# A new order of one turn in a two-layer Mamba, expert and attention kernel: feed-forward through bank 0, sums later, row transfers one by one

## What is computed

```python
xn = layernorm(x)
x = x + mamba(xn) + experts(xn)          # layer 0
xn = layernorm(x)
x = x + attention(xn) + swiglu_ffn(xn)   # layer 1

# mamba, per channel i (256) and state n (16)
hs, gate = split(xn @ in_proj.T)
u  = silu(conv4(hs) + conv_b)
dt, B, C = rmsnorm of the three parts of u @ x_proj.T      # 64, 16, 16 wide
dt = softplus(dt @ dt_proj.T + dt_b)
h[t, i, n] = exp(dt[t, i] * A[i, n]) * h[t-1, i, n] + dt[t, i] * u[t, i] * B[t, n]
y[t, i]    = sum over n of h[t, i, n] * C[t, n]
out = ((y + u * D) * silu(gate)) @ out_proj.T
# experts: the best one of 8 per token, 128 -> 512 -> 128 with relu
# attention: 16 heads of 8, window +-32; ffn: 128 -> 384 -> 128, silu(gate) * up
```

## Time and profile before

| | |
|---|---|
| time, median of 3 runs | 1080.61 us (1080.15 to 1082.40) |
| span of the profiled execution | 1078.4 us |
| busy in it: PE / DVE / ACT / POOL | 81% / 75% / 59% / 38% |
| turn 4 (scan 0 at 578.88 us, next turn's 109.05 us later): PE / DVE busy | 95 / 91 us |

### The profile page before, as it was taken

How to read it: one execution, slowest core, us unless ns; L and a number is a source line. 1 busy time by engine, 2 the same in 40 slices (tenths; PEclk the granted TensorE clock), 3 DMA queues, 4 the chain that set the end, 5 groups by cost and what they waited for, 6 DMA issues and landing times.

```text
span 1078.4 us, 14023 instructions
## 1 busy us (share of the span) xinstructions
...
## 2 busy tenths in 40 slices
...
DMA packets 85945, 123.09 MB, mean 114 GB/s; under 512 B 8560, under 2 KB 43760, under 8 KB 85744
## 3 DMA queue, kind: packets, MB, share of 16 engines
...
...
## 4 chain that ended last, share of the span: by engine, by line
PE 41%; DVE 30%; issue 13%; POOL 10%; ACT 4%; DMA 2%; SPq 0%; DVEq 0%; POOLq 0%
PE y_bank L1279 11%; DVE hst L801 10%; DVE dBu L793 5%; POOL hc L1190 3%; POOL xs_d L1158 3%; PE work L1297 3%; PE more L1398 3%; POOL x_res L1174 3%; DVE nmax L946 2%; PE work L1444 2%; PE work L1380 2%; DVE dc L863 2%; PE work_l L1380 1%; PE work L1410 1%; DVE fsg L955 1%
## 5 line engine op out<-in xcount | busy, mean ns | idle before, releaser
L1190 POOL TENSOR_TENSOR hc<-hst,bcr 128x1024 f32<-128x1024 f32 x116 | 277.6, 2393 | 507.2 <-DVE dBu L793 447.8
L1279 PE MATMUL y_bank<-hc,pk 128*128 128x512 f32 x512 | 261.4, 635 | 61.6 <-POOL hc L1190 48.1
L801 DVE TENSOR_TENSOR_SCAN hst<-dA,dBu 128x1024 f32<-128x1024 f32 x128 | 291.5, 2278 | 14.5 <-issue 12.6
L793 DVE TENSOR_TENSOR dBu<-dtu,bcr 128x1024 f32<-128x1024 f32 x128 | 176.3, 1377 | 15.4 <-DMA bcr<-bc_d 2.0
L1016 ACT ACTIVATE dA<-dt,neg_a 128x511 f32<-128x511 f32 x256 | 171.1, 727 | 9.3 <-DVE hst L801 8.0
L1279 PEld LDWEIGHTS y_bank<-hc,pk 128*128 128x128 f32 x512 | 92.3, 195 | 161.5 <-issue 77.9
L1101 ACT COPY pT<-more 96x512 f32<-96x512 f32 x120 | 69.8, 582 | 87.8 <-PE more L1398 87.6
L1398 PE MATMUL more<-pk,pexp 128*96 128x128 f32 x480 | 94.2, 292 | 21.0 <-ACT pexp L1088 16.2
L1398 PEld LDWEIGHTS more<-pk,pexp 128*96 128x96 f32 x480 | 57.8, 130 | 90.3 <-issue 71.2
L1088 ACT ACTIVATE pexp<-work,nmax 128x96 f32<-128x96 f32 x240 | 78.2, 339 | 15.4 <-DVE nmax L946 15.4
L1088 ACT ACTIVATE pexp<-work_l,nmax 128x96 f32<-128x96 f32 x240 | 78.1, 339 | 4.0 <-DVE nmax L946 3.8
...
## 6 DMA issues: line engine op xcount, KB each, us to landing
bcr<-bc_d SPq DMA_DIRECT2D x128, 512.0 KB
...
```

The source lines that it names most:

```text
L793: v.tensor_tensor(dBu[:], dtu[par], bcr[n % RING][:, 0:1, :].to_broadcast([P, NH, L]), ALU.mult).then_inc(s_dBu, 1)
L801: v.tensor_tensor_scan(hst[n % 2][:].rearrange("p h t -> p (h t)"), dA[n % 2][:].rearrange("p h t -> p (h t)"), dBu[:].rearrange("p h t -> ...
L1190: g_.tensor_tensor(hc[n % 2][:], hst[n % 2][:], bcr[n % RING][:, 1:2, :].to_broadcast([P, NH, L]), ALU.mult).then_inc(s_hc, 1)
L1279: last = t.matmul(y_bank[h][:], ident, hc[n % 2][:, h, :], start=False, stop=(n == N - 1))
```

## The change

The tables of the list are written anew and some units are split.

- `ffn` becomes `fg` (PE gate matmul and ACT tanh), `fs` (DVE), `fu` (PE up matmul) and `fh` (DVE), one slot or more apart, in slots 17 to 23 instead of three whole units at slots 12, 17 and 21. All six matmuls of a sequence go through bank 0 instead of the layer-1 banks; a new helper and a longer `take0` keep the order between them and the `pre` units.
- `zg0` and `zg1` go from slots 4 and 6 to slots 10 and 11, `sg0` and `sg1` to the heads of slots 11 and 12.
- `xdbl` to `dw` come earlier: `xdbl` slot 7 (was 9), `ss` slot 8 (10), `xdr` and `bc` slot 9 (12, 13), `dtT` 13 (16), `dtp0` 14 (18), `dtp1` 15 (19), `drl0`/`drl1` at the heads of 15 and 16 (19, 21), `de` 17 (22), `dw` 19 (23). `dt` moves from 25 to 24.
- A scan step is split into `step` (scan) and `product` (DVE `dBu`, POOL `hc`). Five units stand between the two (`MID`): `slots` at 3, `ss` at 8, `dw` at 19, `dt` at 24, `dtu` at 26.
- Steps 3 and 4 are one slot earlier (4 and 6). `sum` m now stands two slots after its step; for most m that is where it was, for m = 0, 9 and 12 one slot later, for m = 3 one earlier.
- `rows` is split: SP's load and DVE's copy of indices (`slots`) at slot 3, and the four indirect transfers at slots 5, 7, 9 and 11 instead of all at slot 10.
- `th0` is separated from `hs0` and moved behind the decays on ACT.

```diff
-PRE_AT = {0: ['xnT', 'hs0'], 2: ['u0'], 3: ['hs1'], 4: ['zg0', 'u1'], 6: ['sg0', 'zg1'], 7: ['sg1'], 9: ['xdbl'], 10: ['ss'], 12: ['xdr'], 13: ['bc'], 16: ['dtT'], 18: ['dtp0'], 19: ['drl0', 'dtp1'], 21: ['drl1'], 22: ['de'], 23: ['dw'], 24: ['dln'], 25: ['dt'], 26: ['dtu'], 27: ['start']}
-FFN_AT = {12: 0, 17: 1, 21: 2}
+HEAD = {11: [("pre", "sg0", 0)], 12: [("pre", "sg1", 0)], 15: [("pre", "drl0", 0)], 16: [("pre", "drl1", 0)],
...
+MID = {3: [("scan", "slots", 0)], 8: [("pre", "ss", 0)], 19: [("pre", "dw", 0)], 24: [("pre", "dt", 0)], 26: [("pre", "dtu", 0)]}
...
+SUM_LAG = 2
...
         def take0(eng, b, key):
             before(eng, s_free0, b * L0_N + L0_USES.index(key))
+            at = BANK0.index(("pre", key))
+            lane, last = BANK0[at - 1]
+            a = b - LAG["attn"] + LAG["pre"] - (at == 0)
+            if lane == "attn" and 0 <= a < B:
+                done1(eng, a, FFN_KEY[last])
...
-                elif name == "ffn":
-                    for j, key in enumerate((f"gate{k}", f"up{k}")):
-                        take1(pe, b, key)
-                        t.matmul(w1k(b, key)[:], ffn[:, j, k * P:(k + 1) * P], xn1T[:, WIN:WIN + L], start=True,
-                                 stop=True).then_inc(s_full1, 1)
+                elif name in ("fg", "fu"):
+                    key, j = (f"gate{k}", 0) if name == "fg" else (f"up{k}", 1)
+                    take1(pe, b, key)
+                    if b < B - 1:
+                        pre_done(pe, b, f"{name}{k}")
+                    t.matmul(w1k(b, key)[:], ffn[:, j, k * P:(k + 1) * P], xn1T[:, WIN:WIN + L], start=True,
+                             stop=True).then_inc(s_full1, 1)
...
                     if name == "sum":
-                        if k:
-                            sum_y(b, k - 1)
+                        sum_y(b, k)
```

113 lines of the change are left out of this document (67 added, 46 removed).

## The result

The changed kernel takes **1138.6 us** (1136.7 to 1139.3), the kernel before 1080.4 (1080.2 to 1082.4): ratio 1.0535, 95% interval 1.052 to 1.055. The forecast was 1093.6 with 1070 to 1110. Slower was right, the size was not: 58 us are lost where 13 were forecast.

A forecast was written before the change was run, and what follows sets the result against it. PE early, POOL's transfer block mid-turn and DVE late were taken to bound the kernel. Six turns at +2.6 us (+15.5) and turn 7 at -2.5 gave +13.0 on the span, so 1093.6 us, range 1070 to 1110.

The forecast's parts named there:

- What bounds the kernel: In a full turn of 109.05 us: PE early, POOL's transfer block in the middle, DVE with some waits late.
- Start to scan 5: Scan 3 fills DVE's 3.73 us wait, `dBu` 4 waits for its rows, and PE loses 1.4 us at `sum` 3.
- `xdbl`, `ss`, scan 7: `ss` waits 5 us for `xsq`, PE has gaps of 1.8 and 2.9 us, scan 7 comes 7.1 us late.
- Scan 7 to 9: Without POOL's block this stretch takes 14.8 us instead of 17.69, a gain of 2.9.
- Scan 9 to the next scan 0: Before 50.86 us; faster `dw` and `dc` against changed unit counts and waits, together a gain of 1.6 us.
- The sum: A full turn +4.2 - 1.6 = +2.6 us, six times +15.5, with turn 7 -2.5: span +13.0 us.
- turn 7: The turn without `ss` and `zg`: fewer block and `fs` waits against a later `bcr` 5, -2.5 us.
- The open term: `x_res` (256 KB) between `bcr` 4 and 5 delays `dBu` 4 by 0 to 1.4 us a turn; taken as 0.
- "Faster": Rival: the chain to scan 7 breaks somewhere, for instance `xsq` earlier, and the gains decide; 1063 us, chance 0.25.
- "Slower still": Rival: PE's clock halves after the gaps ahead of `sum` 5, +1.5 to 2 us a turn; 1104 us, chance 0.18.

The follow-up runs named there:

- e3: The kernel before, its order otherwise unchanged, with the four row transfers one by one at slots 10, 11, 13 and 15: 1049.3 us.
- e13: The changed kernel with matmuls of zeros on PE at two places only, ahead of `scores` 0 and `sum` 5: 1121.9 us.
- e1: The changed kernel with matmuls of zeros on PE ahead of eight units in turns 2 to 7: 1099.3 us.
- e14: e1 with `ss` behind `dBu` 6 and `y_out`, and the zeros of `scores` 0 and `sum` 5 moved to `turn` 0 and 4: 1103.1 us.
- e15: e3 with `xdbl`, `ss`, `xdr` and `bc` at the changed kernel's earlier places: 1075.0 us.
- e8: The kernel before with row transfers at slots 10, 12, 15, 17, index copy at slot 8, and `de` and `dw` moved: 1049.3 us.
- e12: e8 with the late part of the turn much as in the changed kernel, the feed-forward whole: 1042.5 us.
- e10: The kernel before, order unchanged, with matmuls of zeros on PE ahead of `sum` 7 and `turn` 13: 1074.5 us.
- e16: e3 with the feed-forward in halves through bank 0: 1054.5 us.
- e2: The changed kernel with the `x_res` load, the index copy and the four row transfers back in a block at slot 10: 1143.5 us.

## Why the prediction was right or wrong

**What bounds the kernel.** PE early, POOL's block in the middle: e3 shows the latter, and more of it than I had thought. Without the block the old order is 32 us faster: scan 7 to 9 takes 12.5 us there instead of 17.7 (e3). My 14.8 kept 2.9 of these 5.2 us, and the changed kernel kept 2.0: both `drl` now stand in this stretch, and DVE waits 3.11 and 2.22 us for ACT ahead of them.

**Start to scan 5.** The mechanism was right, and the size nearly: `dBu` 4 at 20.8 us after scan 0 (20.1 forecast), PE's gap at `sum` 3 2.02 (1.4).

**`xdbl`, `ss`, scan 7.** The mechanism is in the trace step by step: gaps of 1.70 and 2.82 us (1.8 and 2.9 forecast), `ms` 0.31. But `xdbl` ends 35.35 us after scan 0, not 32.8: `sum` 3 and `v2` ran at half clock, 0.9 and 0.8 us, and the gap was 0.6 longer. So `ss` waits 6.94, not 5, and scan 7 comes at 51.6, not 47.6. Of the 4.0 us some 2.5 are `xdbl`'s delay and 1.5 the clock just ahead of scan 7 (e13). Without falls the size was right: scan 7 comes at 47.6 to 47.9 us in turns 2, 3, 5 and 6 of e1. What I made of it was too narrow, though. I blamed the place of `ss`, and with `ss` behind `y_out` at full clock scan 7 is only 0.6 to 1.9 us earlier (e14): `rr`, `xdr` and `sg` wait for the same late work. e15 shows the chain in the old order.

**Scan 7 to 9.** 15.7 us, forecast 14.8.

**Scan 9 to the next scan 0.** Forecast 49.25, measured 51.9: `dw` and `dc` take 0.67 and 1.23 us, as computed. In e8 and e12, which have that gain in the old order, most turns take 49.5 to 50.0 us here, those of e3 50.9 to 52.0. At full clock the stretch is 47.3 (e1), better than forecast. The 4.7 us between are three falls, behind gaps of PE of 1.33, 1.36 and 1.70 us ahead of `turn` 6, 11 and 14. My sum has waits of this kind only as DVE sees them (1.4, 1.6, 1.1, 1.2), priced at their length. **That is the step that failed**: a wait was worth its own length, the fall of PE's clock that may follow stood at nothing in the sum, and a rival priced it at one place only, with 1.5 to 2 us a turn. The runs show 7 us a turn at five places, 39 us in all.

**The sum.** Forecast +2.6 us a turn. At full clock +2.1 (112.7 against 110.6); as it ran +9.2 (119.8). The term that was mis-sized is the clock: nothing in the sum, 7 us a turn in the runs. The rest is small: turn 7 and what follows lost 0.8 where I had a gain of 2.5, and the start lost 2.8 where I had 0 (ahead of turn 1 the profiled executions of all kernels here differ by up to 7 us, 240.6 to 248.0, which was not followed).

The old order pays for its clock too, so +2.1 is not the price of the waits alone: e1 against e10 is 24.8 us, with one fall a turn left in e10 and the zeros' own time in e1. And e3 has the split transfers too: against its 1049.3 us the new order at full clock (1099.3) still loses 50 us, in the main to waits. Scan 7 is 7.6 us later in a usual turn (47.8 against 40.2), scan 7 to 9 takes 3.3 more, and the rest of the turn 3.6 to 4.7 less. So the change is a gain of 32 us, a loss of some 50 in waits and one of 39 in clock. The 50 hold the zeros' own time and the falls of turn 1, and e3 has a fall a turn of its own, so they are rough. Which of the moved units makes the 50 is open in part: e15 has 26 (its own falls included) and e16 5, and moving `zg`, steps 3 and 4 and the sums was not tried by itself in the old order.

**The open term.** 0, as taken. SP's rows show `x_res` between the two loads:

```profile
621.71 0.39 SPq L603 DMA_DIRECT2D bcr<-bc_d  x1
622.16 0.45 SPq L659 DMA_DIRECT2D x_res<-in_hidden  x1
```

`dBu` 4 starts 5.87 us after the first, against 5.7 in turn 7. e2, where `x_res` is loaded later, is the nearer comparison: 5.3 to 5.8 us in turns 2 to 6 there, 5.6 to 5.9 in the kernel after. The Trainium skill (DMA: Bandwidth & Descriptors, "Issuing engines are not separate DMA queues") says that transfers interleave on the same 16 DMA engines; of the 1.4 us that I had allowed for that, the traces show 0.2.

**The rivals.** "Faster" broke where I said: `xsq` was later, not earlier. Its gains were there, though: the split transfers alone made the old order 32 us faster. "Slower still" was the right kind, at one place of five.
